# A graph layer with symmetrised adjacency: two rows added by one VectorE instruction, degree scaling and z on GpSimd, y transposed in half tiles

## The reference, cut to what matters

```
Ws  = 0.5 * (W + transpose(W))            # 8 x 2048 x 2048
A   = sigmoid(U @ U.T)                    # one gate for all graphs
K   = Ws * A
deg = maximum(K.sum(-1), 1e-12)
d   = rsqrt(deg)
K   = K * d[:, :, None] * d[:, None, :]
y   = w_scale * einsum('bnm,bmc->bnc', K, x)
out = layernorm(x + y)                    # over the 64 features
```

## Time and profile before

| what | value |
|---|---|
| time, median of 3 runs | 492.47 us |
| lowest and highest run | 489.37 and 500.56 us |
| the profiled execution, its own time | 489.78 us |
| span of the profiled execution, first to last instruction | 487.9 us |
| mean granted TensorE clock | 0.971 |

### The profile page before, as it was taken

How to read it: one execution, slowest core, us unless ns; L and a number is a source line. 1 busy time by engine, 2 the same in 40 slices (tenths; PEclk the granted TensorE clock), 3 DMA queues, 4 the chain that set the end, 5 groups by cost and what they waited for, 6 DMA issues and landing times.

```text
span 487.9 us, 14490 instructions
## 1 busy us (share of the span) xinstructions
PE 447.6 (92%) x5318; PEld 236.5 (48%) x5318; DVE 417.0 (85%) x1154; ACT 209.9 (43%) x655; POOL 113.4 (23%) x133
## 2 busy tenths in 40 slices
PE   7888899999989999999999999799998999899893
PEld 6556344555435553565354554454445544455352
DVE  6897467899699988999899998799889998799745
ACT  3886232554335442554335532454434542444420
POOL 0000011003330225103330234103330225103452
PEclk9996699999999999999999999999999999989998
DMA  8999299986999799996999699976999689984012
GB/s 290 387 330 350 81 362 368 359 301 221 358 343 324 259 321 362 375 326 236 362 380 358 212 380 364 351 241 244 387 345 343 261 322 361 356 253 170 2 41 47
DMA packets 101387, 143.11 MB, mean 293 GB/s; under 512 B 35824, under 2 KB 35824, under 8 KB 101360
## 3 DMA queue, kind: packets, MB, share of 16 engines
q1 hardware_dynamic: 86496, 139.01, 80.7%
q10 hardware_dynamic: 14864, 3.74, 3.6%
HBM read 138.54 MB, written 4.19 MB: 293 GB/s over the span
## 4 chain that ended last, share of the span: by engine, by line
PE 61%; DMA 14%; DVE 12%; issue 8%; ACT 2%; SPq 1%; POOL 0%; DVEq 0%; POOLq 0%
PE yp L437 35%; DMA k<-in_adj_dram 14%; PE tw L395 10%; PE kt L395 9%; DVE k L666 6%; DVE k L677 3%; PE yp L535 3%; PE yp L470 2%; ACT k L559 1%; ACT gate L546 1%; SPq L251 1%; DVE deg_parts L677 1%; DMA h<-in_L_gnn_U_dram 1%; PE kt L481 1%; PE kt L535 0%
## 5 line engine op out<-in xcount | busy, mean ns | idle before, releaser
L559 ACT ACTIVATE k<-kt 128x512 f32<-128x512 f32 (+3 forms) x288 | 149.5, 524 | 234.1 <-PE kt L395 233.8
L437 PE MATMUL yp<-k,z 128*64 128x512 f32 x944 | 239.6, 615 | 4.9 <-DVE z L697 2.6
L666 DVE TENSOR_TENSOR k<-tw,k 128x512 f32<-128x512 f32 (+2 forms) x320 | 193.4, 604 | 41.9 <-PE tw L395 28.5
L677 DVE CUSTOM_DVE_ANT_0 k<-k,gate 128x512 f32<-128x512 f32 (+2 forms) x320 | 198.5, 620 | 0.0
L395 PEld LDWEIGHTS kt<-ident,k 64*128 64x128 f32 x1920 | 75.4, 142 | 86.3 <-issue 86.1
L395 PEld LDWEIGHTS tw<-ident,k 64*128 64x128 f32 x2176 | 83.5, 141 | 67.0 <-issue 65.7
L395 PE MATMUL kt<-ident,k 64*128 64x64 f32 x1920 | 94.2, 232 | 19.5 <-DVE deg_parts L677 13.5
L395 PE MATMUL tw<-ident,k 64*128 64x64 f32 x2176 | 101.7, 230 | 4.5 <-DMA k<-in_adj_dram 1.7
L437 PEld LDWEIGHTS yp<-k,z 128*64 128x64 f32 x944 | 56.4, 137 | 73.1 <-issue 60.0
L327 POOL TENSOR_TENSOR d<-deg,minus_half 128x4 f32<-128x4 f32 x32 | 32.5, 1015 | 222.1 <-DVE deg L687 221.4
L559 ACT ACTIVATION_READ_ACCUMULATOR k<-kt 128x1 f32 x288 | 57.2, 198 | 0.0
(11 more groups left out here) (53 smaller groups left out, 138.7 us busy)
## 6 DMA issues: line engine op xcount, KB each, us to landing
k<-in_adj_dram SPq DMA_DIRECT2D x128, 1024.0 KB, 7.4
xt<-in_x_dram ACTq DMA_DIRECT2D x7, 512.0 KB, 7.6
out_dram<-h SPq DMA_DIRECT2D x7, 512.0 KB, 7.0
xt<-in_x_dram SPq DMA_DIRECT2D x1, 512.0 KB, 14.5
out_dram<-k SPq DMA_DIRECT2D x2, 128.0 KB, 2.1
out_dram<-k SPq DMA_DIRECT2D x3, 64.0 KB, 1.7
h<-in_L_gnn_U_dram SPq DMA_DIRECT2D x1, 128.0 KB, 3.2
out_dram<-k ACTq DMA_DIRECT2D x1, 64.0 KB, 1.9
```

Of the source, the lines that this page charges most:

```text
L437: t = pe.matmul(yp[at:at + C, m // 2, :], z[:, n * G + c, :], K[(n, m)][:, c, :], start=(q == first_unit[m] and c == 0), stop=(q == last_u ...
L559: nc.scalar.activation(K[(j, i)][:, r, c0:UW].rearrange("p (c h e) -> p c h e", h=2, e=H), whole_rows(kt[:, 0:2, :], r % 2, (UW - c0) // P ...
L666: nc.vector.tensor_tensor(row, whole_rows(tw[:, tw_bank[g] // 2 * 2:tw_bank[g] // 2 * 2 + 2, :], g % 2, w // P), row, ALU.add).then_inc(su ...
L677: nc.vector.tensor_tensor_reduce(row, row, A[:, A_AT[g]:A_AT[g] + w], 1.0, 0.0, ALU.mult, ALU.add, deg_parts[:, i * G + r, j:j + 1]).then_ ...
```

## The change

Three edits, with the row numbers of all other steps as they were:

1. In the six steps off the diagonal, one VectorE instruction adds two neighbouring rows (128 x 1024) and counts `sum_done` by two. The gate products stay one for each row. The order on VectorE becomes add rows g and g+1, gate row g-1, gate row g.
2. The scaling and clipping of the degrees goes from VectorE to GpSimd, in front of the power there, and z is made on GpSimd right behind it, at the rows of `DEG_ROWS` (before: on VectorE at `Z_ROWS`).
3. y of a graph is transposed at one place, row 68, in sixteen half-tile transposes instead of twice four full ones at rows 66 and 68. The halves of a block lie in two banks, so `scale_y` now works by halves, and the first one, still at row 66, waits for the whole of it.

```diff
             def add_x(b, k):
-                pool.wait_ge(y_scaled, 2 * b + (2 * k // LN_PARTS + 1))
+                pool.wait_ge(y_scaled, 2 * b + (k % 2 + 1))
...
             def degrees(b, k):
+                pool.wait_ge(deg_summed, NZ * b + (k + 1))
+                s = slice(*Z_GROUPS[k][:2])
+                pool.sem_inc(deg_taken, 1)
+                nc.gpsimd.tensor_scalar(deg[:, s], deg[:, s], 0.5, DEG_EPS, ALU.mult, ALU.max).then_inc(deg_ready, 1)
                 pool.wait_ge(deg_ready, NZ * b + (k + 1))
-                s = slice(*Z_GROUPS[k][:2])
                 nc.gpsimd.tensor_tensor(d[:, s], deg[:, s], minus_half[:, s], ALU.pow).then_inc(d_ready, 1)
 
+            def make_z(b, k, first):
+                pool.wait_ge(d_ready, NZ * b + (k + 1))
+                pool.wait_ge(x_loaded, b * 16 + 16)
+                if not first:
+                    pool.wait_ge(prod_done, b * NQ + (LAST_PAIR_OF_Z[k] + 1 - NQ))
+                n0, n1, _ = Z_GROUPS[k]
+                nc.gpsimd.tensor_tensor(z[:, n0:n1, :], xt[:, n0:n1, :], per_row(d, n0, n1),
+                                        ALU.mult).then_inc(z_ready, 1)
...
-            def transpose_y(b, k):
-
-                pe.wait_ge(y_copied, 2 * b + (k + 1))
-                for c in range(G):
-                    t = pe.transpose(yp[:, k, c * P:(c + 1) * P], y_sb[:, k, c * P:(c + 1) * P], ident[:, :])
-                t.then_inc(yt_done, 1)
+            def transpose_y(b):
+
+                pe.wait_ge(y_copied, 2 * b + 2)
+                pe.sem_inc(banks_taken, 1)
+                transpose_halves([yp[:, h, :] for h in range(2)], 0,
+                                 [y_sb[:, k, c * P:(c + 1) * P] for k in range(2) for c in range(G)]).then_inc(yt_done, 2)
...
                     for lag in range(lags):
-                        for k in range(2):
-                            if due(row, lag, Y_ROWS[k]):
-                                transpose_y(b - lag, k)
+                        if due(row, lag, Y_ROWS[1]):
+                            transpose_y(b - lag)
...
+            def add_two_rows(b, g):
+                s, r = LOWER[g]
+                rows = K[STEPS[s]][:, r:r + 2, :].rearrange("p r (c h e) -> p (r c) h e", h=2, e=H)
+                if r == 0:
+                    dve.wait_ge(loaded[STEPS[s]], b * 16 + 16)
+                dve.wait_ge(tw_done, b * NL + (g + 2))
+                pair = tw[:, tw_bank[g] // 2 * 2:tw_bank[g] // 2 * 2 + 2, :].rearrange("p h (c e) -> p c h e", e=H)
+                nc.vector.tensor_tensor(rows, pair, rows, ALU.add).then_inc(sum_done, 2)
...
                 nc.vector.tensor_reduce(deg[:, n0:n1], deg_parts[:, n0:n1, :], AX_X, ALU.add).then_inc(deg_summed, 1)
-                dve.wait_ge(deg_summed, NZ * b + (k + 1))
-                nc.vector.tensor_scalar(deg[:, n0:n1], deg[:, n0:n1], 0.5, DEG_EPS, ALU.mult,
-                                        ALU.max).then_inc(deg_ready, 1)
-
-            def make_z(b, k, first):
-
-                n0, n1, _ = Z_GROUPS[k]
-                dve.wait_ge(d_ready, NZ * b + (k + 1))
-                dve.wait_ge(x_loaded, b * 16 + 16)
-                if not first:
-                    dve.wait_ge(prod_done, b * NQ + (LAST_PAIR_OF_Z[k] + 1 - NQ))
-                nc.vector.tensor_tensor(z[:, n0:n1, :], xt[:, n0:n1, :], per_row(d, n0, n1),
-                                        ALU.mult).then_inc(z_ready, 1)
...
-            def scale_y(b, k):
-                if k == 0:
+            def scale_y(b, half):
+                if half == 0:
                     dve.wait_ge(f_ready, b + 1)
                     dve.wait_ge(h_moved, b * 16 + 16)
-                dve.wait_ge(yt_done, 2 * b + (k + 1))
-                src = yp[:, k, :].rearrange("p (c half e) -> p half c e", c=G, half=2)
-                fk = f[:, 8 * k:8 * k + 8].rearrange("p (half c) -> p half c", half=2).unsqueeze(3)
-                dst = h[:, 8 * k:8 * k + 8, :].rearrange("p (half c) e -> p half c e", half=2)
+                    dve.wait_ge(yt_done, 2 * b + 2)
+                src = yp[:, half, :].rearrange("p (k c e) -> p k c e", k=2, e=C)
+                fk = f[:, :].rearrange("p (k h c) -> p k h c", k=2, h=2)[:, half, :, :].unsqueeze(3)
+                dst = h[:, :, :].rearrange("p (k h c) e -> p h k c e", k=2, h=2)[:, half, :, :, :]
...
                 for g in range(NL):
-                    add_row(b, g)
+                    if STEPS[g // G][0] == STEPS[g // G][1]:
+                        add_row(b, g)
+                    elif g % 2 == 0:
+                        add_two_rows(b, g)
```

More of the change, by code:

```diff
@@ L67 @@
 PRODUCT_ROWS = [29, 29, 32, 32, 33, 33, 35, 35, 38, 38, 39, 39, 42, 44, 44, 45, 45, 45, 46, 46, 46, 47, 50, 52, 54, 56, 56, 56, 59, 61, 64, 65]
+FIRST_PRODUCT_ROWS = [29, 29, 32, 32, 33, 33, 35, 35, 38, 38, 39, 39, 42, 44, 44, 45, 45, 45, 46, 46, 46, 47, 50, 52, 54, 56, 56, 56, 59, 61, 64, 65]
 DEG_ROWS = [25, 32, 40, 43]
-Z_ROWS = [26, 35, 43, 44]
+FIRST_DEG_ROWS = [25, 32, 40, 43]
 KEEP_ROW = 55
@@ L218, in bass_graph_resnorm_kernel @@
         banks_taken = sem("banks_taken")
-        deg_summed, deg_ready, d_ready, z_ready = sem("deg_summed"), sem("deg_ready"), sem("d_ready"), sem("z_ready")
+        deg_summed, deg_taken, deg_ready = sem("deg_summed"), sem("deg_taken"), sem("deg_ready")
+        d_ready, z_ready = sem("d_ready"), sem("z_ready")
         prod_done, y_copied, yt_done = sem("prod_done"), sem("y_copied"), sem("yt_done")
@@ L324, in degrees, with beside @@
             def degrees(b, k):
+                pool.wait_ge(deg_summed, NZ * b + (k + 1))
+                s = slice(*Z_GROUPS[k][:2])
+                pool.sem_inc(deg_taken, 1)
+                nc.gpsimd.tensor_scalar(deg[:, s], deg[:, s], 0.5, DEG_EPS, ALU.mult, ALU.max).then_inc(deg_ready, 1)
                 pool.wait_ge(deg_ready, NZ * b + (k + 1))
-                s = slice(*Z_GROUPS[k][:2])
                 nc.gpsimd.tensor_tensor(d[:, s], deg[:, s], minus_half[:, s], ALU.pow).then_inc(d_ready, 1)
+            def make_z(b, k, first):
[6 more added lines that the diff above has]
+                                        ALU.mult).then_inc(z_ready, 1)
             def beside_row(b, row):
                 pool.wait_ge(lower_done, b * NL + row)
-            def beside(b, row, lag):
+            def beside(b, row, lag, first):
                 for k in range(NZ):
-                    if due(row, lag, DEG_ROWS[k]):
+                    if due(row, lag, (FIRST_DEG_ROWS if first else DEG_ROWS)[k]):
                         degrees(b, k)
+                        make_z(b, k, first)
                 for k in range(LN_PARTS):
@@ L352, in steps @@
                     for lag in range(lags - 1, -1, -1):
-                        beside(b - lag, row, lag)
+                        beside(b - lag, row, lag, lags - lag == 1)
             steps(0, 1)
@@ L361, in _ @@
                     degrees(B - 1, k)
+                    make_z(B - 1, k, False)
             for k in range(LN_PARTS):
@@ L485, in products_at @@
                 for at in range(NQ * G):
-                    if due(row, lag, PRODUCT_ROWS[at]):
+                    if due(row, lag, (FIRST_PRODUCT_ROWS if first else PRODUCT_ROWS)[at]):
                         product(b, at // G, at % G, first)
@@ L704, in scale @@
                 nc.vector.tensor_scalar(f[:, :], d[:, :], ws[:, 0:1], 0.5, ALU.mult, ALU.mult).then_inc(f_ready, 1)
-            def scale_y(b, k):
-                if k == 0:
+            def scale_y(b, half):
+                if half == 0:
                     dve.wait_ge(f_ready, b + 1)
                     dve.wait_ge(h_moved, b * 16 + 16)
-                dve.wait_ge(yt_done, 2 * b + (k + 1))
-                src = yp[:, k, :].rearrange("p (c half e) -> p half c e", c=G, half=2)
-                fk = f[:, 8 * k:8 * k + 8].rearrange("p (half c) -> p half c", half=2).unsqueeze(3)
-                dst = h[:, 8 * k:8 * k + 8, :].rearrange("p (half c) e -> p half c e", half=2)
+                    dve.wait_ge(yt_done, 2 * b + 2)
+                src = yp[:, half, :].rearrange("p (k c e) -> p k c e", k=2, e=C)
+                fk = f[:, :].rearrange("p (k h c) -> p h k c", k=2, h=2)[:, half, :, :].unsqueeze(3)
+                dst = h[:, :, :].rearrange("p (k h c) e -> p h k c e", k=2, h=2)[:, half, :, :, :]
                 nc.vector.tensor_tensor(dst, src, fk.broadcast_to([P, 2, G, C]),
@@ L739, in beside @@
                 for k in range(NZ):
-                    if due(row, lag, DEG_ROWS[k]):
+                    if due(row, lag, (FIRST_DEG_ROWS if first else DEG_ROWS)[k]):
                         sum_degrees(b, k)
-                    if due(row, lag, Z_ROWS[k]):
-                        make_z(b, k, first)
                 if due(row, lag, SCALE_ROW):
@@ L832, in _ @@
                     sum_degrees(B - 1, k)
-                if Z_ROWS[k] >= NL:
-                    make_z(B - 1, k, False)
             for k in range(2):
```

## The result

| | median (lowest to highest), runs |
|---|---|
| after | 496.07 us (490.61 to 505.97), 12 |
| before | 492.03 us (483.14 to 501.16), 12 |

The ratio is 1.0156, with a 95% interval of 1.0106 to 1.0205: slower by about 1.6%. Medians here are over all runs; ratios leave out runs that were disturbed, so that ratio and medians need not agree to the last tenth. The profiled execution of after took 497.24 us (span 495.4 us), that of before 489.78 us: 7.5 us more.

The account below looks back on a forecast made before the run. A graph's 54 us were taken as about 33 us of TensorE, 5 of a transfer and 15 of VectorE. Terms 3.7 + 2.0 - 1.0 + 0.3 gave +5.0 us on 489.8, so 494.8 us; range 483 to 502.

Parts of the forecast that it names:

- The decisive place, row 28: VectorE's add at row 28 waits for the load of unit (3, 2) and has no slack; TensorE's row 30 follows.
- The four passages that I priced at 0.92 us: Graph changes where the transfer comes last at row 28: 0.39 us later release plus 0.53 us add, 3.7 us in all.
- the three with cover: The other three graph changes, with some slack before row 28's add and TensorE's row 30: 0.67 us each, 2.0 us.
- some cover is left: Slack in three graph changes: 0.11 us before row 28's add, about 0.14 us before TensorE at row 30.
- What is given back: Later groups get z sooner, so one TensorE wait of 1.02 us at 135.93 should go: -1.0 us.
- 0.1 us is won and lost again: With y in half tiles the first product starts at about 273.0 instead of 273.12, but row 30 loses it again.
- The end of the kernel: At the very end z of group 2 is on the path, 0.2 us more work and 0.1 waiting: +0.3 us.
- z on GpSimd at no cost: Row 27's gate product may stand behind GpSimd's z, 0 to 0.25 us a graph; taken as 0.
- ScalarE's square 0.5 us later: Centring, variance power and divisions queue behind z on GpSimd, delaying the square about 0.5 us; VectorE's variance comes later, no cost.
- the savings get through: Rival: unit (3, 2) doesn't come last, so 1.2 us a graph is saved, -8 us, 482 us; chance 0.25.
- nothing reaches the end: Rival: transfers are the limit and the wait is only moved, 490 us; chance 0.12.
- The loss of TensorE's clock: Rival: longer waits at rows 18, 22 or 30 lower the clock, five passages pay 1.5 us, 502.3 us; chance 0.18.

Follow-up runs that it names:

- run 8: The changed kernel with only the gate product of row 27 moved ahead of the double add of rows 28 and 29: 489.91 us, ratio 0.9970 to before.
- runs 1 to 5: Before plus double adds (497.59 us), y halves (497.86), or GpSimd scaling and z (1.0271); after with gate products first (0.9952), or double adds in steps' first halves (1.0079).
- run 7: The kernel before, single adds, with the gate product of a step's last row ahead of the next step's first add, no other edit: 482.51 us, ratio 0.9885.
- runs 6 and 9 to 12: After: double adds only in steps' last halves (0.9984), no double adds (1.0164), y as before (1.0125); before, gate first, double adds: with y halves (1.0028), without (0.9969).
- run 9: The changed kernel with single adds everywhere, without the double adds: 496.59 us, ratio 1.0164 to before.
- run 10: The changed kernel with y transposed as before, double adds and GpSimd work kept: 494.83 us, ratio 1.0125 to before.
- run 3: The kernel before with only scaling and z moved to GpSimd: 498.12 us, ratio 1.0271 to before.
- run 11: The kernel before with double adds, y in halves and each step's last gate product first, z and scaling on VectorE: 490.76 us, ratio 1.0028.

## Why the prediction was right, point by point

- **The decisive place, row 28: shown.** The waits, the chain, and run 8, which mends this place alone and takes the whole loss away (1.0156 to 0.9970).
- **Its size: 5.7 us foretold, 6.7 measured as waiting at row 30, 7.6 as delay from row 29 to row 32, but 5.3 in all up to the last graph's row 32.** The four passages that I priced at 0.92 us added 0.54 to 0.95 us of waiting each, 2.9 us together instead of 3.7 (in the one at 109 us the trace of before shows no wait for the transfer, so only three are sure); the three with cover, at 0.67 us, added 1.05 to 1.53, 3.75 us instead of 2.0. These errors partly cancel, which is luck. The step that failed in size is "some cover is left": the add at row 28 stands idle in all seven, since TensorE and VectorE reach it sooner after the release of (3, 2). Counted from that release a passage became longer by 0.21 to 0.53 us in six of the seven; I had 0.53 us for row 28 where the transfer comes last. The double add itself, 1.13 us from start to start (268.94 to 270.07), was priced rightly at 1.14.
- **What is given back: -1.0 us foretold, -2.3 measured** outside row 29 to 32. All of TensorE's 2.6 us of waiting for z in the steady part went, its 0.46 us among them. Most of that isn't won: it comes back at row 30, as I had it for the transposes of y ("0.1 us is won and lost again"), where it is about 0.7 us in the graph of the earlier trace rows.
- **The end of the kernel: +0.3 us foretold, +2.2 measured.** 0.5 us is the wait for z, the other 1.7 are TensorE's clock in the last stage. These don't follow the edits: the same 52 products took 10.7 to 10.9 us in the profiles of runs 1 to 5, 7 and 8, of which run 7 has none of the edits, and 9.25 in those of runs 6 and 9 to 12, of which run 9 and run 10 have two each.
- **Scaling on GpSimd** 0.3 us taken, 0.24 measured. **Double add, y's transposes:** 96, and 0.70 us where I had 0.75. **VectorE's busy time:** 400 us foretold, 397.1 measured.
- **z on GpSimd at no cost: right in this kernel, for a reason that I hadn't seen.** I priced only what the gate product loses beside GpSimd. The other direction costs 1.08 us a graph (run 3), and in the changed kernel it doesn't arise for the group that counts, because double add and `scale_y` stand there instead. Where one edit is undone the other cost comes: 1.0164 without the double adds, 1.0156 with them. So the term is right for the three edits together and would be wrong for z with single adds.
- **ScalarE's square 0.5 us later, "no cost": right in time, wrong in size.** In the graph of the earlier trace rows the square starts 2.73 us after the copy before it instead of 1.72, so 1.0 us later. VectorE's degree sum for group 3 waits 2.41 us for ScalarE in six of the eight graphs (all degree sums together 23.6 us, 10.3 before), and no wait of TensorE over 0.2 us follows it for some 13 us in five of the six, 8 us in the other.
- **The rivals.** That the savings get through fell, by the waits at row 28. That nothing reaches the end fell with it. The loss of TensorE's clock isn't what made the steady part slower: waits of 1.0 us at row 30 and one of 2.16 us at 266.29 cost none (the 16 transposes behind it take 0.71 us). One wait of 2.60 us did, as its row and the window behind it show (1.03 us for the 16 transposes, clock 0.53). Before had two such places, and one behind a wait of 2.21 us, so after lost less by the clock here, not more; after, then before:

```profile
378.30 1.03 PE L411 MATMUL kt<-ident,k 64*128 64x64 f32 x16 [2.60 <-DVE deg_parts L701]
...
380.00:382.00 2.00, 2.00 (x22) 0.84 (x20) 1.03 (x4) 0.63 (x3) 0.00 (x0) 0.53 0.71 228
```

```profile
427.98 0.72 PE L395 MATMUL kt<-ident,k 64*128 64x64 f32 x16 [2.21 <-DVE deg_parts L677]
428.63 1.98 PE L437 MATMUL yp<-k,z 128*64 128x512 f32 x4
```

The forecast of 494.8 us was for the profiled execution, which took 497.24, 7.5 us more than before instead of 5.0. As a ratio the forecast is 1.010, just below the measured interval. The mechanism, the place and the sign were right. Up to the last graph's row 32 it was 4.7 us foretold (3.7 + 2.0 - 1.0) and 5.3 measured, closer than its parts; the rest is the end of the kernel, and 1.7 us of it the clock.

## What to carry to other kernels

Merging two instructions of an in-order engine delays what stood between them: look for who waits for that, and move it ahead of the merged one. Here that reordering by itself (run 7) won more than any of the three edits. Before work goes to GpSimd, look at what VectorE starts at the same moments, in both directions; and don't add up edits measured alone, since each sets what the others run beside.

## What was not expected of the hardware

- GpSimd is held by VectorE as well as the other way: beside a gate product (two inputs in SBUF) that starts with it, a power of 128 x 4 takes 1.57 us instead of 1.03, and a multiply of 128 x 256 takes 1.14 instead of 0.61. Each is longer by some 0.54 us, most of the 0.68 us of a gate product. Beside a double add and `scale_y`, which read PSUM, nothing of this is seen (1.03 and 0.61 us).
- A multiply of 128 x 256 takes 0.61 us on GpSimd and 0.41 on VectorE (run 11), 1.5 times. The Trainium skill (GPSIMD Engine Reference, "Performance versus the Vector engine") has nearly 2 for a large elementwise add; the small one here is nearer.
- The clock in the last stage differs between profiled executions of kernels whose work there is the same, 9.25 us in six profiles, before among them, against 10.7 to 10.9 in eight: some 1.6 us of a profiled execution is such scatter. What decides it stays open.
